# Six part products in a new order, expert weights turned one expert at a time, and 64-row key matmuls

## The reference

```
x = x + 0.5 * experts(layernorm(x))
x = x + attention(layernorm(x))
x = x + 0.5 * experts(layernorm(x))
```

## Time and profile before

| | us |
|---|---|
| median of 3 runs | 971.23 (966.93 to 976.51) |
| the profiled execution | 967.66 |
| its span | 965.9 |
| busy: PE / PEld / DVE / ACT / POOL | 636.5 / 516.7 / 504.7 / 297.2 / 235.6 |
| expert layer 0, first gather to last scatter issued | 96.4 to 225.9 |
| attention's parts and first loads | 227.6 to 311.9 |
| attention's steps, outputs and projection | 311.9 to 751.7 |
| expert layer 1, first gather to last scatter issued | 833.4 to 957.3 |

### The profile page before, as it was taken

One profiled execution on the slowest core, in us unless ns is written; L12 is line 12 of the kernel. 1 busy time (PEld: TensorE's weight loads), 2 busy tenths in 40 slices (PEclk: granted clock), 3 DMA queues, 4 the chain that ended last, 5 costly groups with the idle time before them and its releaser, 6 DMA issues.

```text
span 965.9 us, 29195 instructions
## 1 busy us (share of the span) xinstructions
PE 636.5 (66%) x12366; PEld 516.7 (53%) x12366; DVE 504.7 (52%) x1712; ACT 297.2 (31%) x473; POOL 235.6 (24%) x227
## 2 busy tenths in 40 slices
PE   4512998700733789888898879899972811689640
PEld 3501556500422678777787768788862800357430
DVE  7977222123721567565666557667766777512120
ACT  2390454300522232323232313232332264063210
POOL 2000738884533000000000000014110000346864
PEclk9999999955885599999898979999985555599985
DMA  4272213325355332323222323234342506112322
GB/s 122 59 218 80 53 17 43 34 24 142 132 160 173 92 62 70 59 69 60 69 44 74 52 70 56 65 72 97 75 110 46 175 1 178 24 35 31 45 25 22
DMA packets 99163, 73.27 MB, mean 76 GB/s; under 512 B 26569, under 2 KB 92258, under 8 KB 98914
## 3 DMA queue, kind: packets, MB, share of 16 engines
q1 hardware_dynamic: 85858, 57.01, 23.4%
q0 software_dynamic: 13184, 14.43, 9.2%
HBM read 44.34 MB, written 27.01 MB: 74 GB/s over the span
## 4 chain that ended last, share of the span: by engine, by line
PE 38%; DVE 15%; POOL 14%; issue 11%; ACT 9%; SPq 6%; DMA 5%; DVEq 0%; ACTq 0%; POOLq 0%
PE banks L1002 10%; ACT arena L778 8%; PE banks L1005 7%; POOL x_mid L554 5%; PE banks L1025 5%; POOL out_dram L554 5%; SPq L469 3%; DVE arena L1119 3%; PE banks L1066 2%; PE banks L849 2%; POOL arena L543 2%; PE banks L929 2%; PE banks L913 1%; DMA out_dram<-arena 1%; SPq L440 1%
## 5 line engine op out<-in xcount | busy, mean ns | idle before, releaser
L778 ACT ACTIVATE arena<-banks 128x1024 f32<-128x1024 f32 x96 | 98.3, 1024 | 263.4 <-PE banks L1025 263.4
L1002 PE MATMUL banks<-arena 128*128 128x32 bf16 x3072 | 126.8, 194 | 42.8 <-issue 16.1
L1002 PEld LDWEIGHTS banks<-arena 128*128 128x128 bf16 x3072 | 112.4, 101 | 68.1 <-ACT arena L778 38.7
L1366 DVE TRANSPOSE_TENSOR_REDUCE arena<-banks 128x32 f32<-128x1024 f32 x96 | 120.0, 1250 | 18.1 <-PE banks L1005 13.8
L1005 PE MATMUL banks<-arena 128*128 128x32 bf16 x3072 | 108.6, 178 | 8.6 <-issue 8.6
L1005 PEld LDWEIGHTS banks<-arena 128*128 128x128 bf16 x3072 | 93.6, 97 | 11.3 <-issue 11.3
L543 POOL DMA_INDIRECT arena<-table,arena x64 | 61.5, 961 | 126.2 <-DVE arena L1276 107.7
L607 POOL COPY arena<-arena 128x576 f32 (+1 forms) x8 | 5.3, 668 | 329.6 <-PE banks L1056 329.6
L1382 DVE TENSOR_REDUCE arena<-banks 32x8 f32<-32x64 f32 (+1 forms) x96 | 20.1, 209 | 107.9 <-PE banks L1017 107.8
L710 ACT ACTIVATE arena<-banks,arena 128x512 f32<-128x512 f32 x64 | 44.0, 687 | 85.2 <-PE banks L929 85.2
L1025 PE MATMUL banks<-arena 128*128 128x64 bf16 x1536 | 64.4, 198 | 0.7 <-issue 0.7
(11 more groups left out here) (182 smaller groups left out, 1021.4 us busy)
## 6 DMA issues: line engine op xcount, KB each, us to landing
query_parts<-arena SPq DMA_DIRECT2D x8, 768.0 KB, 6.4
arena<-query_parts SPq DMA_DIRECT2D x16, 384.0 KB
table<-arena SPq DMA_DIRECT2D x2, 2176.0 KB, 9.4
arena<-in_L_ffn_fc2s_dram SPq DMA_DIRECT2D x4, 1024.0 KB, 10.8
arena<-query_parts SPq DMA_DIRECT2D x16, 256.0 KB
key_parts<-arena SPq DMA_DIRECT2D x8, 384.0 KB, 7.0
arena<-key_parts SPq DMA_DIRECT2D x8, 384.0 KB
head_outputs<-arena SPq DMA_DIRECT2D x128, 18.0 KB
```

Of the source, the lines that this page charges most:

```text
L778: nc.scalar.activation(dst, psum[:, 2 * r:2 * r + 2, :].rearrange("p u (h n) -> p u h n", h=H), ACT.Exp, scale=HD ** -0.5).then_inc(s_prob, 1)
L1002: pe.matmul(sc[:, :, 2 * a:2 * a + 2], rel_k[:, y:y + P], q_st[:, r, :, q0 + 2 * a:q0 + 2 * a + 2], start=(a == 0), stop=False, skip_group ...
L1366: step(v.tensor_reduce(mp, psum[:, 2 * (s % 3):2 * (s % 3) + 2, :].rearrange("p u (h n) -> p (u h) n", n=32), AX.X, ALU.max, apply_transpo ...
```

## The change

The order of the six products of parts is reversed within each run, so that a run's query parts are 0, 1, 2 and its key parts 2, 1, 0 (key parts are stored in reverse). The query loads thereby read consecutive parts instead of one part repeated. PE turns the weights of expert e+1 behind `first_half(e)`, and those of expert 0 ahead of everything; ACT copies them behind the gelus of expert e. `second_half(e)` comes in the same turn as `first_half(e)`. POOL gathers 4 experts ahead instead of 5, and clears nothing. DVE clears rows 32 to 63 of `k_st` at the head of `attention()`, and the key matmuls use rows 0 to 63. The eight ACT copies into `q_st` stand behind the last expert. The diff, cut to its core:

```diff
-        Q_PART = (0, 0, 0, 1, 1, 2)
-        K_PART = (0, 1, 2, 0, 1, 0)
+        Q_PART = (0, 1, 2, 0, 1, 0)
+        K_PART = (2, 1, 0, 1, 0, 0)
...
-                    q = qs[c, Q_PART[a], 0:HD, :, bass.ds(pr * PT, PT)]
-                    q = q.unsqueeze(0).to_broadcast([b - a, HD, H, PT])
-                    k = ks[0:b - a, :, :, bass.ds(pr * PT, PT)].rearrange("w d h n -> (w d) h n")
+                    q = qs[c, 0:b - a, :, :, bass.ds(pr * PT, PT)].rearrange("w d h n -> (w d) h n")
+                    k = ks[3 - (b - a):3, :, :, bass.ds(pr * PT, PT)].rearrange("w d h n -> (w d) h n")
...
+        def weights_read(n, k):
+            return 2 + n * (NAB + NXB) + NXB + k
...
-                return k_part[:, i // 2 % 2, w, :]
+                return k_part[:, i // 2 % 2, 2 - w, :]
...
-                AHEAD = 5
+                AHEAD = 4
...
-                    elif n == 0 and e < E - 1:
-                        q, i = 2 * H // 4, e - (E - AHEAD)
-                        pool.memset(k_words[32:64, q * i:q * i + q], 0.0).then_inc(s_zero, 1)
-                        pool.memset(k_words[64:P, q * i:q * i + q], 0.0).then_inc(s_zero, 1)
-                        pool.wait_ge(s_zero, 2 * i + 2)
...
-                for k in range(NWB):
-                    act.wait_ge(s_tr, tr + NXB + k + 1)
-                    ...
+                def weights(e):
+                    k = tr + NXB + 3 * e
+                    act.wait_ge(s_tr, k + 1)
+                    nc.scalar.copy(w1T[:, e, :], tr_bank(k)).then_inc(s_trf, 1)
+                    act.wait_ge(s_tr, k + 2)
+                    nc.scalar.copy(w2T[:, e, :, :],
+                                   tr_bank(k + 1).rearrange("p (c d) -> p c d", c=NC)).then_inc(s_trf, 1)
+
+                weights(0)
                 for e in range(E):
                     ...
-                    if n == 0:
-                        if e == 0:
-                            ...
+                    if e + 1 < E:
+                        weights(e + 1)
+                if n == 0:
+                    act.wait_ge(s_tab, 16)
+                    act.wait_ge(s_const, 9)
+                    for e in range(E):
                         nc.scalar.copy(q_words[96:P, 4 * e:4 * e + 4],
                                        parity[96:P, :].unsqueeze(1).to_broadcast([32, 4, PT // 2])).then_inc(s_parity, 1)
...
-                for k in range(NWB):
-                    bank, e = bank_of(NXB + k), k // 2
-                    ...
+                def turn_weights(e):
+                    for w in range(2):
+                        if w and e:
+                            pe.wait_ge(s_yT, n * E + e)
+                        else:
+                            pe.wait_ge(s_trf, weights_read(n, 2 * e))
+                        bank = tr_bank(tr + NXB + 3 * e + w)
+                        for c in range(NC):
+                            src = raw2[:, e, P * c:P * c + P] if w else raw1[:, e, c, :]
+                            last = pe.transpose(bank[:, P * c:P * c + P], src, ident)
+                        last.then_inc(s_tr, 1)
 
                 def turn_rows(e):
                     pe.wait_ge(s_rows[e], 64 * (n + 1))
-                    bank = bank_of(NWB + NXB + e)
+                    pe.wait_ge(s_trf, weights_read(n, 2 * e + 1))
+                    bank = tr_bank(tr + NXB + 3 * e + 2)
...
+                turn_weights(0)
                 turn_rows(0)
                 for e in range(E):
                     first_half(e)
                     if e + 1 < E:
+                        turn_weights(e + 1)
                         turn_rows(e + 1)
-                    if 0 < e < E - 1:
-                        second_half(e - 1)
-                    if e >= E - 2:
-                        second_half(e)
+                    second_half(e)
...
-                            last = pe.matmul(sc[:, h], k_st[:, r, h, L * b + P * kb:L * b + P * kb + P],
-                                             q_st[:, r, h, q0:q0 + 32],
+                            last = pe.matmul(sc[:, h], k_st[0:64, r, h, L * b + P * kb:L * b + P * kb + P],
+                                             q_st[0:64, r, h, q0:q0 + 32],
...
                 rows_in(0)
-                for e in range(1, E + 1):
-                    if e < E:
-                        rows_in(e)
-                    if e >= 2:
-                        scale(e - 2)
-                scale(E - 1)
+                for e in range(E):
+                    if e + 1 < E:
+                        rows_in(e + 1)
+                    scale(e)
 
             def attention():
+                dve.wait_ge(s_tab, 16)
+                v.memset(k_words[32:64], 0.0).then_inc(s_zero, 1)
```

More of the change, by code:

```diff
@@ L444, in attention @@
                             sp.wait_ge(s_pst[b], 16)
-                        sp.wait_ge(s_zero, 8)
+                        sp.wait_ge(s_zero, 1)
                     if i >= 4 and loads:
@@ L711, in expert_layer @@
                                              bias=b1T[:, e * NC + c:e * NC + c + 1]).then_inc(s_g, 1)
-                    if n == 0:
-                        if e == 0:
-                            act.wait_ge(s_tr, tr + NAB)
-                            act.wait_ge(s_tab, 16)
-                            act.wait_ge(s_const, 9)
+                    if e + 1 < E:
[4 more added lines that the diff above has]
+                    for e in range(E):
                         nc.scalar.copy(q_words[96:P, 4 * e:4 * e + 4],
@@ L837, in bank_of @@
                 def bank_of(k):
-                    read = 2 + n * (NAB + NXB) + k - 1
-                    if k < NAB + 2:
-                        pe.wait_ge(s_trf, read)
+                    pe.wait_ge(s_trf, 2 + n * (NAB + NXB) + k - 1)
                     return tr_bank(tr + k)
@@ L986, in attention @@
                 pe.wait_ge(s_rv, 16)
-                pe.wait_ge(s_zero, 8)
+                pe.wait_ge(s_zero, 1)
                 pe.wait_ge(s_parity, E)
@@ L1300, in rows_in @@
                 def rows_in(e):
-                    k = NWB + NXB + e
+                    k = NXB + 3 * e + 2
                     dve.wait_ge(s_tr, tr + k + 1)
```

## The result

The changed kernel takes **1027.13 us** (median of 4 runs, 1018.19 to 1031.82) against 969.08 of the kernel before on the same chip (964.37 to 976.51): a ratio of 1.058, 95% interval 1.047 to 1.069. The forecast was 955, and the range ended at 984. The profiled execution took 1031.7, its span is 1030.0, 64.1 more than before.

| stretch | before | after | change | predicted |
|---|---|---|---|---|
| start to last scatter of layer 0 | 224.3 | 210.2 | -14.1 | -14.8 |
| from there to the first score matmul | 87.6 | 70.0 | -17.6 | -20 |
| steps, first to last score matmul | 390.2 | 495.1 | **+104.9** | +31 - 2 |
| from there to the last index matmul of layer 1 | 142.4 | 141.8 | -0.6 | 0 |
| from there to the last scatter | 111.2 | 102.9 | -8.4 | -9.1 |

A forecast was written before the change was run, and what follows sets the result against it. Bounds were taken as POOL in the expert layers, no engine in the parts stage, PE and ACT in turns in the score steps. Terms -9.1 - 14.8 - 20 - 2 + 31 = -15 gave 955 us, range 922 to 984.

The forecast's parts named there:

- the last sentence on the query loads: Steps of scores: later pairs' loads run under PE work, and PE's one stop for stores queued behind them goes, -2 us.
- C: Steps of scores: breaks at 64-row blocks also slow each key matmul from 0.024 to 0.04 us; +34, 1005 us; chance 0.14.
- Weights one at a time: Expert layers: turning weights expert by expert lets the first scatter start 12.0 us earlier in each layer.
- Four gathers ahead: Expert layers: four scatters instead of three have a gather behind them, 2.9 us more in each layer.
- No memsets: Layer 0: POOL's dropped memsets save 5.7 us; DVE's new memset, at most 9.6 us, falls into idle time and costs nothing.
- Query loads of the first pair: Parts stage: query loads of consecutive parts spread over more DMA engines, so the scores start earlier, -20 us.
- Rival D: Parts stage: query loads are not faster, held by DRAM or the queue; +7, 978 us; chance 0.13.
- 64 rows: Steps of scores: changing row counts around key matmuls costs 0.16 us a block, 192 blocks, +31 us.
- Rival B: Steps of scores: the 64-row key matmuls cost no breaks; -46, 925 us; chance 0.20.

The follow-up runs named there:

- e9: The changed kernel with five gathers ahead instead of four, nothing else; 1027.78 us in one run.
- e4: The kernel before with only the new order of the products and its query loads; 1019 us, ratio 1.047 to the kernel before.
- e12: The changed kernel, 64 rows kept, with a later pair's nine loads issued one per step of scores instead of all at once; 946 us, ratio 0.978.
- e7: The changed kernel with key matmuls on 128 rows and a later pair's nine loads issued one per step; 912 us, ratio 0.941 to the kernel before.
- e1: The changed kernel with its key matmuls on 128 rows again, DVE clearing rows 32 to 127; 996 us, ratio 1.019 to the kernel before.
- e5: The kernel before with only the key matmuls put on 64 rows; 999 us, ratio 1.026 to the kernel before.
- e10: Old order of products and 128-row key matmuls, every query load cut into one load a term (8 partitions), all fifteen in a burst; 1004 us (989 to 1016).
- e8: The changed kernel with 128-row key matmuls and one unused row behind each query part in DRAM, so loads use few DMA engines; 945 us, ratio 0.976.

## Why the prediction was wrong

**The step that failed** is the last sentence on the query loads: "Later loads run under PE work; PE's one stop for stores queued behind them, 1.91 at 396.53, goes: -2." I asked whether somebody waits for the data of these loads, and nobody does. I did not ask who else uses the DMA engines, and PE's own instructions come through them. The stop of 1.91 did go: ACT waits 4.3 us for stores of head outputs in the steps before and not at all after. But the term was -2 and measured +62.4 by the stops, and some 8 to 13 us more by what the stops do to the clock (below). The profile before held the warning: PE already had 26.6 us of stops by issue in the steps, for which I gave no cause, and the page's table of DMA queues lists one for instructions. The spread that I counted as the gain of the parts stage was the cost of every later pair, for 7 pairs against one. None of the four rivals had this mechanism; the slower one (C) was about the 64-row blocks.

Point by point:

*Weights one at a time:* right. Scatter 0 starts 17.9 and 17.7 us behind the last index matmul, 16.8 predicted, 28.8 before. The missing microsecond is the clock: in 921.0 to 926.5 the granted clock is 0.65, low (1.2 GHz) for a part of it and high (2.4) behind, and `first_half(0)` loses 1.8, where I allowed 0.8 and named 3 as the bound.

*Four gathers ahead:* right. +2.9 predicted for each layer; e9 gives 3.0 and 3.3.

*No memsets:* right. First to last scatter in layer 0 went from 88.1 to 84.9, -3.2, against 2.9 - 5.7 = -2.8. DVE's memset takes 6.88 (bound 9.6) and lies in the idle time where I put it; this is its row:

```profile
197.97 6.88 DVE L1321 MEMSET arena<- 32x8192 f32 x1 [1.76 <-issue]
```

*Query loads of the first pair:* right in kind, 2.4 short. -17.6 against -20, and -17.8 in e4, where it is nearly alone. ACT's waits for stores did not go under 2 us, and the first scores come 32.5 behind the first load (247.61) instead of 28. Rival D is refuted.

*64 rows:* right. 31 predicted for 192 blocks at 0.16. The medians of the breaks give 0.096 + 0.079 = 0.175 a block, 33.6; e12's steps are 31.6 longer than e7's; e1 against the changed kernel gives 31 in medians and 38 by ratios, e5 25 in medians. Rival B (free) is refuted. So is C: two keys are 25 ns apart as before, and the blocks cost 0.17, not 0.24. The Trainium skill (TensorEngine Tiling (Array Packing), Key Properties) has it that a change of the tiling mode drains the engine; the 0.096 on entering and 0.079 on leaving agree.

With the failed term taken out, the measured terms are -14.1 - 17.6 - 0.6 - 8.4 + 31.6 = -9 in place of my -13 for the same parts: 960 for the median. e12, in which the burst is gone, took 946; there the steps also lost 12 us of stops that the kernel before already had (30.5 to 18.1, start to start).

*The rest of the steps.* The +104.9 are about +62 of stops, -4 of waits for other engines, and +46 of busy time of PE. The breaks are 34 to 37 of these 46 (33.6 by the medians above; PE's busy time in e12 beside e7 is 36.6 longer). The other 10 to 12 are the clock. These rows (busy by stretch, columns as in rows 4) are the steps of e12 and of the changed kernel, which differ in the pacing of the loads alone:

```profile
279.00:689.11 410.11, 374.82 (x10510) 326.27 (x10511) 250.97 (x627) 114.06 (x124) 19.96 (x35) 0.93 0.34 65
```

```profile
280.12:775.69 495.57, 387.88 (x10511) 336.50 (x10511) 250.74 (x627) 114.06 (x124) 19.90 (x35) 0.84 0.40 54
```

The same matmuls take 13.1 us more of busy time, with a mean granted clock of 0.84 in place of 0.93. From e7 to e1 it is 12.3 (0.93 to 0.84), from the kernel before to e4 7.8 (0.92 to 0.85). Around the stops of 461.97 to 488.89 the granted clock is 1.00 in 458 to 461, 0.50 from 466 to 492 although PE works for 9.4 us of it, and 1.00 again from 496 on. So a stop is paid twice, as idle time and as matmuls at the lower level (1.2 GHz) behind it.

## What to carry to other kernels

A load for which nobody waits can still hold up an engine that only needs its next instructions: where PE shows idle time "by issue" in the middle of ready work, set the windows of the load queue beside those of the instruction queue. Spread loads are right where their data is waited for; where they run ahead, issue them one at a time, paced by the work they run under (here 81 to 84 us for an edit of a few lines). And a part product that saves rows but changes the number of rows between neighbours pays for it, here about 0.17 us a block, and gains nothing.

## What the runs showed of the hardware

- With the load queue at 100% of 16 engines, and also at 55% (e10, 466 to 478), PE gets no instructions in time and stops for up to 9.4 us (10.7 in e1). Where the same loads come one by one, 30.1% over 37 us in e7, or over few engines, 28.7% over 26 us in e8, the stops of the steps are 19.2 and 28.9 us together, about those of the kernel before (26.6). The packet of instructions itself is only a little slower: in 470.5 to 472.0 one took 7.9% of 16 x 1.5 us = 1.9 us, against 1.3 as a mean over the span (0.8% of 16 x 1030 / 102). Most of the delay is that it starts late.
- PE can run out of instructions without any load beside it: in e7 it stops for 2.19 us before 425.34, with no data packet in 423.2 to 425.3, and again a packet of instructions landed 1.3 us before it goes on.
- A burst makes the loads themselves slower. The steps move 21.76 MB by the load queue in both kernels; its packets take 34.9% of 495 us = 173 us of all 16 engines after, 26.1% of 390 = 102 before, and 28.2% of 410 = 116 in e12, with the same spread loads one by one. In the stretch of 463.0 to 470.5 all engines are busy at 108 GB/s, while the traffic of the parts stage reaches 347 GB/s at 0.99 in 238 to 239, so 108 is no limit of the engines.
- The same loads at the old width keep SP's queue longer: the nine loads of a pair are issued in 8 us in the changed kernel (460.59 to 468.7) and in 28 in e8 (342.67 to 371.1), so width also sets how long SP is held from its stores.
